# Layer 1 of a two-layer kernel: B and C rows spread by transfers, two PSUM banks for y, one fp32 product for the step size, the last state column kept by GpSimd

## The reference

```python
x = silu(depthwise_conv_5x5(x) + conv_b)
xs = x.reshape(B, C, L)                                   # L = 3136
x_dbl = einsum('kd,bdl->bkl', x_proj_w, xs)
dts, Bs, Cs = x_dbl[:, :6], x_dbl[:, 6:10], x_dbl[:, 10:]  # R = 6, N = 4
delta = softplus(einsum('dr,brl->bdl', dt_w, dts) + dt_b)
log_dA = maximum(delta[:, :, None] * A[None, :, :, None], LOG_EPS)
P = exp(cumsum(log_dA, axis=-1))
dB_u = delta[:, :, None] * Bs[:, None] * xs[:, :, None]
hs = P * cumsum(dB_u / maximum(P, 1e-9), axis=-1)
y = einsum('bdnl,bnl->bdl', hs, Cs) + xs * Ds
```

## Time and profile before

| | |
|---|---|
| median of 3 runs | 4351.19 us (4345.33 to 4353.54) |
| the profiled execution's own time | 4340.87 us |
| its span | 4339.1 us |
| TensorE busy | 3840.0 us (88%) |
| VectorE busy | 3258.9 us (75%) |
| ScalarE busy | 2790.3 us (64%) |
| GpSimd busy | 2263.5 us (52%) |
| mean granted TensorE clock | 0.913 of 2.4 GHz |

### The profile page before, as it was taken

How to read it: one execution, slowest core, us unless ns; L and a number is a source line. 1 busy time by engine, 2 the same in 40 slices (tenths; PEclk the granted TensorE clock), 3 DMA queues, 4 the chain that set the end, 5 groups by cost and what they waited for, 6 DMA issues and landing times.

```text
span 4339.1 us, 74865 instructions
## 1 busy us (share of the span) xinstructions
PE 3840.0 (88%) x22806; PEld 2793.4 (64%) x22806; DVE 3258.9 (75%) x5219; ACT 2790.3 (64%) x4796; POOL 2263.5 (52%) x1928
## 2 busy tenths in 40 slices
PE   6999999999999999887888889888888888898877
PEld 6787878888787878675555545545545555455432
DVE  3767666676767675605988978879879889789899
ACT  1545455454636363657887877878778778778775
POOL 0323223232323242405776867767768677677787
PEclk9999999999999999987997988979979979889877
DMA  7565555556464644373423324424324334243100
GB/s 233 146 186 150 174 161 160 174 147 183 135 196 124 212 123 142 80 184 82 109 71 92 103 57 106 115 51 109 98 61 108 79 81 109 61 108 92 37 20 22
DMA packets 314879, 507.44 MB, mean 117 GB/s; under 512 B 190000, under 2 KB 255248, under 8 KB 314144
## 3 DMA queue, kind: packets, MB, share of 16 engines
q1 hardware_dynamic: 314432, 502.08, 42.3%
HBM read 424.94 MB, written 77.07 MB: 116 GB/s over the span
## 4 chain that ended last, share of the span: by engine, by line
PE 22%; DVE 12%; issue 9%; ACT 7%; POOL 5%; DMA 1%; DVEq 1%; ACTq 0%; POOLq 0%; SPq 0%
PE ps_front L1313 6%; PE ps_y L1386 5%; DVE ps_q L1080 5%; DVE h L1107 5%; PE ps_front L1306 3%; PE ps_prep L1335 2%; POOL u L1000 2%; PE ps_y L1383 2%; POOL h L1011 2%; PE ps_front L1326 1%; PE ps_bc L1356 1%; ACT d_a L1201 1%; DMA out_dram<-y 1%; ACT d_a L1195 1%; ACT y L1221 1%
## 5 line engine op out<-in xcount | busy, mean ns | idle before, releaser
L1011 POOL TENSOR_TENSOR h<-h,c_rows 128x448 f32<-128x448 f32 x672 | 766.7, 1141 | 366.1 <-DVE ps_q L1114 194.6
L522 ACT ACTIVATE act_h<-ps_up,b 128x448 f32<-128x448 f32 x672 | 408.9, 635 | 778.5 <-PE ps_up L640 778.3
L1000 POOL TENSOR_TENSOR u<-dxs,b_rows 128x448 f32<-128x448 f32 x672 | 767.0, 1141 | 48.0 <-ACT b_rows L1209 42.3
L1386 PE MATMUL ps_y<-h,ident 128*128 128x448 f32 x1344 | 733.2, 633 | 35.0 <-POOL h L1011 25.4
L319 POOL TENSOR_TENSOR h_low<-act_h,h_high 128x448 fp32r<-128x448 f32 x224 | 287.7, 1284 | 900.6 <-ACT h_high L527 900.6
L1080 DVE TENSOR_TENSOR_SCAN ps_q<-d_a,q_last,ps_q 128x448 f32<-128x448 f32 x576 | 659.6, 1145 | 13.2 <-ACT d_a L1201 13.2
L1107 DVE TENSOR_TENSOR_SCAN h<-d_a,ps_q 128x448 f32<-128x448 f32 x576 | 648.3, 1126 | 6.5 <-issue 6.2
L1313 PEld LDWEIGHTS ps_front<-win,taps 120*112 120x112 f32 x4608 | 538.4, 188 | 139.8 <-issue 136.4
L613 PE MATMUL ps_stage<-win,taps 124*112 124x112 f32 x6144 | 607.2, 260 | 2.7 <-DVE w_low L366 2.7
L613 PEld LDWEIGHTS ps_stage<-win,taps 124*112 124x112 f32 x6144 | 607.0, 178 | 3.3 <-DVE w_low L366 2.8
L1313 PE MATMUL ps_front<-win,taps 120*112 120x112 f32 x4608 | 550.8, 273 | 7.5 <-ACT win L1151 3.7
(11 more groups left out here) (93 smaller groups left out, 7156.2 us busy)
## 6 DMA issues: line engine op xcount, KB each, us to landing
taps<-in_t_dram SPq DMA_DIRECT2D x192, 896.0 KB, 4.9
taps<-in_t_dram SPq DMA_DIRECT2D x192, 672.0 KB, 4.9
xres<-in_x_dram SPq DMA_DIRECT2D x224, 168.0 KB, 2.5
x_dram<-x1o SPq DMA_DIRECT2D x224, 168.0 KB, 2.0
x1pad<-x_dram SPq DMA_DIRECT2D x96, 392.0 KB, 8.1
out_dram<-y SPq DMA_DIRECT2D x168, 224.0 KB
xpad<-in_x_dram SPq DMA_DIRECT2D x29, 1176.0 KB, 10.4
conv<-in_x_dram SPq DMA_DIRECT2D x3, 1176.0 KB, 14.9
```

The source lines that it names most:

```text
L522: nc.scalar.activation(act_h[u % 2][:, t, :], ps_up[t][:, 0:BT], ACT.Gelu, bias=b1[:, t:t + 1]).then_inc(gelu_done, 1)
L1000: nc.gpsimd.tensor_tensor(u[s % U_SLOTS][:, :], dxs[:, t, :], b_rows[n][:, :], ALU.mult).then_inc(u_done, 1)
L1011: nc.gpsimd.tensor_tensor(h[s % H_SLOTS][:, :], h[s % H_SLOTS][:, :], c_rows[n][:, :], ALU.mult).then_inc(hc_done, 1)
L1386: nc.tensor.matmul(ps_y[:, 0:BT], ident[:, :], h[s % H_SLOTS][:, :], start=False, stop=(n == N - 1)).then_inc(y_added, 1)
```

## The change

- B and C rows: `spread_b`, `spread_c`, `keep_b`, `keep_c`, `sel` and the bank `ps_bc` go. SyncE issues eight transfers a band from `xd` in SBUF to `b_rows` and `c_rows` in SBUF, at the steps at which the products stood. The source pattern repeats each of four rows 32 times. GpSimd waits for the transfers' semaphores. `xd` gets three buffers (`XD_SLOT`), since it is read for longer.
- The step size: `delta_rows` makes z with one fp32 product from `xd`; `high`, `parts` and `split` go.
- `y`: two PSUM banks and two buffers (`Y_SLOTS`), so the first product of a run waits for the copy of the bank of two runs before.
- `h_last` moves from PSUM to SBUF. GpSimd writes it in `times_c` with an add on one column, and waits for it; `keep_h` on VectorE goes.
- Order: `d_a` is made four steps ahead instead of five, in the same six slots. The third `dxs` product of a band moves from step 11 to step 1 of the band itself. In the first two steps of a pass TensorE's front piece stands after the projection. SyncE's and GpSimd's first pass is written out ahead of the loop.

```diff
+DA_LEAD = 4
+Y_SLOTS = 2
+XD_SLOT = (0, 1, 0, 1, 0, 1, 2)
...
-        xd = sb("xd", [XD, BT])
-        high = sb("high", [XD, BT], F32R)
-        parts = sb("parts", [XD, BT], F32R)
+        xd = [sb(f"xd{i}", [XD, BT]) for i in range(max(XD_SLOT) + 1)]
...
+        h_last = sb("h_last", [128, STEPS])
+        y = [sb(f"y{i}", [128, BT]) for i in range(Y_SLOTS)]
...
-        ps_bc = pb("ps_bc")
         ps_q = [pb(f"ps_q{i}") for i in range(2)]
-        ps_y = pb("ps_y")
+        ps_y = [pb(f"ps_y{i}") for i in range(Y_SLOTS)]
         no_q = ps_q[0][:, BT:BT + 1]
-        h_last = ps_q[0][:, BT + 1:BT + 1 + STEPS]
...
-        DXS_AT = (8, 10, 11)
-        SPREAD_B_AT, KEEP_B_AT = (6, 7, 8, 9), (7, 8, 9, 10)
-        SPREAD_C_AT, KEEP_C_AT = (10, 11), (11,)
-        SPREAD_C_NOW, KEEP_C_NOW = {0: 2, 1: 3}, {0: 1, 1: 2, 2: 3}
+        DXS_AT, DXS_NOW = (8, 10), 1
+        LOAD_B_AT, LOAD_C_AT, LOAD_C_NOW = (6, 7, 8, 9), (10, 11), {0: 2, 1: 3}
...
+            def row(b, which, n):
+                first = n * XB + which * GI
+                return xd[XD_SLOT[b]][first:first + GI, :].unsqueeze(1).broadcast_to([GI, CB, BT])
+
+            def load_b(f, b, n, first=False):
+                if first:
+                    sp.wait_ge(xd_ready, 1)
+                else:
+                    sp.wait_ge(u_done, f * S + b * STEPS - N + n + 1)
+                sp.dma_start(b_rows[n][:, :], row(b, 0, n)).then_inc(b_in[n], 16)
+
+            def load_c(f, b, n, first=False):
+                if not first:
+                    sp.wait_ge(hc_done, HC0 + f * S + b * STEPS - N + n + 1)
+                sp.dma_start(c_rows[n][:, :], row(b, 1, n)).then_inc(c_in[n], 16)
...
                     while todo and unit_step[todo[0][2]] <= s + AHEAD:
                         load, k, _ = todo.pop(0)
                         load(g + 1, False, k)
+                    if ahead or b + 1 < BANDS:
+                        if j in LOAD_B_AT:
+                            load_b(f, fb, LOAD_B_AT.index(j))
+                        if j in LOAD_C_AT:
+                            load_c(f, fb, LOAD_C_AT.index(j))
+                    if j in LOAD_C_NOW and not (first and b == 0):
+                        load_c(g, b, LOAD_C_NOW[j])
                     if s >= N + Y_LAG + 1 and (s - N - Y_LAG - 1) % N == 0:
                         store(g, (s - N - Y_LAG - 1) // N)
...
                 if t == 0:
-                    pool.wait_ge(b_kept, g * B_UNITS + b * N + n + 1)
+                    pool.wait_ge(b_in[n], (g * BANDS + b + 1) * 16)
...
                 if t == 0:
-                    pool.wait_ge(c_kept, g * B_UNITS + b * N + n + 1)
+                    pool.wait_ge(c_in[n], (g * BANDS + b + 1) * 16)
                 pool.wait_ge(h_done, g * S + s + 2)
                 if b + 1 < BANDS:
+                    nc.gpsimd.tensor_tensor(h_last[:, s % STEPS:s % STEPS + 1], h[s % H_SLOTS][:, BT - 1:BT],
+                                            zeros[:, 0:1], ALU.add).then_inc(h_kept, 1)
                     pool.wait_ge(h_kept, g * KEPT + s + 1)
...
-            def keep_h(g, s):
-                b, j = s // STEPS, s % STEPS
-                if b + 1 < BANDS:
-                    dve.wait_ge(h_done, g * S + s + 2)
-                    nc.vector.tensor_copy(h_last[:, j:j + 1], h[s % H_SLOTS][:, BT - 1:BT]).then_inc(h_kept, 1)
...
-                nc.scalar.activation(xd[:, :], ps_prep[0][:, 0:BT], ACT.Identity,
-                                     bias=low_rows[:, 1:2]).then_inc(xd_ready, 1)
-                nc.scalar.activation(high[:, :], ps_prep[0][:, 0:BT], ACT.Identity,
-                                     scale=low_rows[:, 0:1]).then_inc(xd_ready, 1)
+                nc.scalar.activation(xd[XD_SLOT[b]][:, :], ps_prep[0][:, 0:BT], ACT.Identity,
+                                     bias=one_rows[:, 0:1]).then_inc(xd_ready, 1)
...
-                    ahead = s + DA_SLOTS - 1
+                    ahead = s + DA_LEAD
...
-                for part in range(2):
-                    mm = nc.tensor.matmul(z[:, 0:BT], dtw[part][:, t, :], parts[:, :],
-                                          start=(part == 0), stop=(part == 1))
-                mm.then_inc(z_done, 1)
+                nc.tensor.matmul(z[:, 0:BT], dtw[:, t, :], xd[XD_SLOT[b]][:, :],
+                                 start=True, stop=True).then_inc(z_done, 1)
...
                 if n == 0:
-                    pe.wait_ge(y_kept, g * RUNS + r + 1)
+                    pe.wait_ge(y_kept, g * RUNS + max(r - Y_SLOTS + 1, 0) + 1)
```

More of the change, by code:

```diff
@@ L93 @@
 XB = 32
-DT0 = 4 * GI
-ONE = DT0 + 2 * R
+DT0 = 2 * GI
+ONE = DT0 + R
 XD = N * XB
@@ L734, in layer1 @@
         xproj = sb("xproj", [128, TILES, XD])
-        dtw = [sb(f"dtw_{part}", [XD, TILES, 128], F32R) for part in ("high", "low")]
-        sel = sb("sel", [XD, 2, 128], F32R)
-        low_rows = sb("low_rows", [XD, 2])
+        dtw = sb("dtw", [XD, TILES, 128])
+        one_rows = sb("one_rows", [XD, 1])
         skip = sb("skip", [128, TILES, 128])
@@ L790, in layer1 @@
         d_a_ready = sem("d_a_ready")
-        b_ready = sem("b_ready")
-        c_ready = sem("c_ready")
+        b_in = [sem(f"b_in{n}") for n in range(N)]
+        c_in = [sem(f"c_in{n}") for n in range(N)]
         clipped = sem("clipped")
@@ L951, in group @@
                 store(g, RUNS - 1)
[L953 to L959, removed]
+            assert last > 1
+            first_slabs(1)
+            for n in range(N):
+                load_b(0, 0, n, True)
+            for n in range(N):
+                load_c(0, 0, n, True)
+            group(0, 2, True)
+            with sp.Fori(1, last - 1) as g:
+                group(g, 2)
+            group(last - 1, 1)
             group(last, 0)
-            sp.wait_ge(y_stored, (groups * RUNS + 1) * 16)
+            for k in range(Y_SLOTS):
+                sp.wait_ge(y_stored[k], (groups * len(range(k, RUNS, Y_SLOTS)) + 1) * 16)
         @block.gpsimd
@@ L967, in _ @@
             nc.gpsimd.memset(log_eps[:, 0:1], -LOG_EPS).then_inc(prepared, 1)
-            pool.sem_inc(y_stored, 16)
+            for k in range(Y_SLOTS):
+                pool.sem_inc(y_stored[k], 16)
             pool.sem_inc(y_kept, 1)
@@ L971, in _ @@
             pool.sem_inc(gated, 1)
-            pool.sem_inc(hc_done, N)
+            pool.sem_inc(hc_done, HC0)
             pool.sem_inc(y_added, H_SLOTS)
             pool.wait_ge(prepared, PREPARED)
[L976 to L982, removed]
             def times_x(f, b, t, first=False):
@@ L1012, in times_c, with group @@
                                         ALU.mult).then_inc(hc_done, 1)
-            def group(g, more):
+            def group(g, more, first=False):
                 for s in range(S):
@@ L1021, in group @@
                         times_c(g, s - 1)
-                    if prepare and j == SPLIT_AT:
-                        split(f, fb)
-                    if prepare and j in DXS_AT[:-1]:
+                    if prepare and j in DXS_AT:
                         times_x(f, fb, DXS_AT.index(j))
+                    if j == DXS_NOW:
+                        times_x(g, b, TILES - 1, b == 0 and first)
+                    if prepare and j + U_AHEAD == STEPS - N:
+                        pool.wait_ge(xd_ready, f * BANDS + fb + 1)
                     if s + U_AHEAD < S:
@@ L1029, in group @@
                         times_b(g + 1, s + U_AHEAD - S)
-                    if prepare and j == DXS_AT[-1]:
-                        times_x(f, fb, TILES - 1)
                 times_c(g, S - 1)
-            split(0, 0, True)
-            for t in range(TILES):
+            for t in range(TILES - 1):
                 times_x(0, 0, t, True)
@@ L1039, in _ @@
                 times_b(0, s, True)
-            if last:
-                with pool.Fori(0, last) as g:
-                    group(g, True)
+            group(0, True, True)
+            with pool.Fori(1, last) as g:
+                group(g, True)
             group(last, False)
@@ L1202, in exp_a @@
                                      bias=LOG_EPS).then_inc(d_a_ready, 1)
[L1204 to L1216, removed]
             def keep_y(g, r):
                 act.wait_ge(y_added, g * S + (r + 1) * N + H_SLOTS)
-                act.wait_ge(y_stored, (g * RUNS + r + 1) * 16)
-                nc.scalar.activation(y[:, :], ps_y[:, 0:BT], ACT.Copy).then_inc(y_kept, 1)
+                act.wait_ge(y_stored[r % Y_SLOTS], (y_uses(g, r) + 1) * 16)
+                nc.scalar.activation(y[r % Y_SLOTS][:, :], ps_y[r % Y_SLOTS][:, 0:BT], ACT.Copy).then_inc(y_kept, 1)
             def group(g, more):
@@ L1347, in delta_rows @@
                 z = z_bank(t)
-                for part in range(2):
-                    mm = nc.tensor.matmul(z[:, 0:BT], dtw[part][:, t, :], parts[:, :],
-                                          start=(part == 0), stop=(part == 1))
-                mm.then_inc(z_done, 1)
[L1353 to L1359, removed]
-                if n == 0:
```

(21 more changed lines are left out.)

105 lines of the change are left out of this document (39 added, 66 removed).

## The result

The changed kernel takes 6717.47 us (median of 4 runs, 6713.65 to 6723.70) against 4348.26 us (4 runs): a ratio of 1.546, with a 95% interval of 1.544 to 1.549. That is 55% slower, far outside my range of 4070 to 4790 us. The forecast said slower, but for another mechanism and with a small part of the size. One of my rivals, a source of four neighbouring rows that gives little more than one engine's rate, had 13% and about 7690 us.

A forecast was written before the change was run, and what follows sets the result against it. VectorE fills some bands now, waits lengthen others; row loads crowding four DMA engines were to bound the changed pass. 7 x (313 - 300.4) = +88, last pass -11; 4340.87 + 77 gives 4418, about 4430 us with 10 for the median; range 4070 to 4790.

The forecast's parts named there:

- the price of a row load: Transfers into `b_rows` and `c_rows`: 2.6 us each, near a store's middle rate, with ends of 2.5 and 3.5 us.
- the rival: Row loads: four engines reading neighbouring rows share one engine's rate, 10 us a load, about 7690 us in all; chance 13%.
- my upper end of 3.5 us: Row loads at a whole store's price, 3.5 us: a pass of 359 us, about 4780 us in all.
- Four engines: Row loads were expected on four DMA engines of 16, the same four as the output stores.
- Crowding on four engines: DMA: row loads add 20.8 us a band to four engines' 162 us a pass; pass 313 us, about 4430; chance 37%.
- my floor without transfers: Second-stage pass without row transfers, after taking off copies, `u` waits and half the `z_log` waits: 266.6 us.
- the `z_log` waits: VectorE's 22.0 us a pass of waits for ScalarE's `z_log`: half, 11 us, given back; ends nothing to 22 us.
- TensorE's clock: Band 0, clock 0.60 of full and TensorE 88% busy: a floor of 45 us put there instead of 51.8.
- The step without `keep_h`: VectorE: dropping the `h_last` copy saves 0.15 us a step, x 72 steps = 10.8 us a pass.
- GpSimd's add: One-column add in 72 of 84 steps: 0.3 us each, GpSimd 33.3 us a band; as bound at 1 us, chance 4%.
- The fp32 step product: TensorE: 21 fp32 step-size products priced like `xproj`'s 23.4 us, against 19.1 us now, so +4.3 us.
- Issues are no bound: SyncE issues eight loads a band among slabs, taps and stores; each wait is met a step or two before.

The follow-up runs named there:

- one_image: Each row transfer of the changed kernel cut in four, one per image, with one source row repeated 32 times, on sixteen engines: 6258.52 us.

## Why the prediction was wrong

**What failed.** The step is the price of a row load, "I take it near the middle rate with a short start: 2.6 us. Ends: 2.5 and 3.5 us". It measured 9.2 us. The nearest row, the store, has the same bytes and engines, but its four engines walk through four blocks of 32 partitions, while a row load's four engines stay for all their packets on four neighbouring partitions. What I set against the rival, "a store's four engines walk four blocks of 32 partitions at once and still move 23 GB/s each", says nothing of readers that stay put: at a pitch of 32 the row loads read the same four blocks, standing still, and got half. So my upper end of 3.5 us was no bound; the rival's 10 us should have been the end of the range.

**The rival.** It had the mechanism and nearly the price (10 us against 9.2; beside it, 229 / 27 is 8.5 us, not 8.4). Its total of 7690 us was too long for two reasons. The price is 46 us of its pass of 722 us. The rest is the engines' other work, 162 us, which it added in full: 514 + 162 = 676 against 599 measured. In the packet records of that pass not every row load pays the full price: some 5,500 of 9,860 packets of 1,792 bytes take 230 to 270 ns, and with the stores' packets they add up to 471 us an engine, where 56 x 8.1 + 75 = 529 were to be expected. That fewer of the four engines share the source while the others carry something else would explain it; it was not tested.

**Four engines.** Right: shares of 0.22 to 0.26 in all runs with four source rows, 0.52 with eight.

**Crowding on four engines.** Right as a mechanism where the sources are apart: 297 us a pass, 4299 us in all. I had 313 and 4430, since my floor without transfers was 266.6 us instead of 250.6. Of these 16 us, 9 are the `z_log` waits that I gave back by half: bands 5 and 6 of a pass without transfers take 35.2 and 35.6 us, where I had 39.3 and 40.2. The rest is mostly band 0, for which I had kept 45 us for fear of TensorE's clock: it takes 39.0 us, at a granted clock of 0.78 of 2.4 GHz instead of 0.60. The granted clock of a pass rose from 0.88 to 0.94 without the transfers, and fell to 0.66 in the changed kernel, whose TensorE waits 272 us for GpSimd's `h`; VectorE bounds the first, the rows the second.

**VectorE, GpSimd, TensorE.** The step without `keep_h` saves 0.11 us rather than 0.15. GpSimd's add takes 0.19 us and starts 0.27 us before the product (I had 0.3). GpSimd was not the bound: in the run without transfers it is busy 222.9 of 250.6 us and waits 19 us for VectorE's `h`. The fp32 step product costs nearly what `xproj` does, as I took it:

```profile
L1336 PE MATMUL ps_prep<-xd,dtw 128*128 128x448 f32 x42 | 28.1, 761 | 0.0
L1323 PE MATMUL ps_prep<-xs,xproj 128*128 128x448 f32 x42 | 25.5, 726 | 0.0
```

(groups of the changed kernel's pass, at its lower clock).

**Issues.** "Issues are no bound" didn't hold in the changed kernel: as shown above, SyncE spent 495 of 599 us in them. It is a consequence of the slow rows, since the same issues take 0.6 us in the median where the sources are apart.

**Left open.** Why a store's engines, whose blocks lie 32 apart, aren't slowed was only argued from their moving; it wasn't tried. The packet records of the stores that run alone in the last pass before the change bear on it: each begins with 18 to 20 packets of over 90 ns, many of 121 to 128 ns, and is mostly at 74 ns after some 1.7 us, while a row load at a pitch of 36 alone has none of over 90 ns. The engines may meet on the same partitions at first and then drift apart, or the write to HBM may start slowly; the records can't tell. Nor was it measured which part of `one_image`'s lead over the changed kernel is due to its rate.

## What to carry to other kernels

When a transfer inside SBUF spreads a few rows, ask two things of its source: how many engines its first dimension gives, and how many distinct groups of partitions they read at one time. Four neighbouring rows gave 25 GB/s to four engines, and one row gave 26 to sixteen. Laying the rows 36 partitions apart, or twice and 12 apart, at no cost in the product that writes them (20.4 us a pass with eight sources and without transfers), took this kernel from 6717 to 4299 and 4095 us. And a price taken from the nearest row holds only if that row has the feature in question. Where no row has it, the case it would make is the end of the range.

## What the runs showed of the hardware

- Row transfers alone: four engines on neighbouring partitions 25 GB/s, sixteen engines on one partition 26, four engines 32 apart 52, four engines 36 apart 102, eight engines 12 apart 199. A packet of 1,792 bytes took 253, 916, 133, 74 and 74 ns.
- While slow row loads stood in the queue, an issue of such a load on SyncE took 3.1 us in the median and 13.6 us at most; with eight sources it took 0.6 us in the median.
- A store with its four blocks in four transfers of 32 rows each was worth 1.6% in the kernel with eight sources, despite four times the issues on SyncE.
- A one-column add on GpSimd takes 0.19 us, and its product starts 0.27 us after it.
